# Count build of a graph network kernel: turns of two tiles in a ring of four one-hot places, tile bounds read in two halves

## What is computed

```
dst = sort(int(3125 * uniform**2)), src = randint(0, 3125)      # 50000 edges
x = layernorm(x + gcn(x))            # 128 -> 512 -> 128, symmetric normalisation
x = layernorm(x + gine(x, edge_attr_32))   # edge MLP input, two batch norms
x = layernorm(x + sage(x))           # two mean aggregations
x = layernorm(x + pna(x))            # 3 layers: max, min, std, var per target, 3 scalers
```

## Time and profile before

| | us |
|---|---|
| median of 3 runs | 3185.71 (3182.45 to 3189.19) |
| the profiled execution | 3187.43 |
| its span, first to last instruction | 3185.6 |
| mean granted TensorE clock | 0.849 |
| count build: first L1620 weight load to last L1641 matmul | 33.06 to 434.6 |

### The profile page before, as it was taken

One profiled execution on the slowest core, in us unless ns is written; L12 is line 12 of the kernel. 1 busy time (PEld: TensorE's weight loads), 2 busy tenths in 40 slices (PEclk: granted clock), 3 DMA queues, 4 the chain that ended last, 5 costly groups with the idle time before them and its releaser, 6 DMA issues.

```text
span 3185.6 us, 49509 instructions
## 1 busy us (share of the span) xinstructions
PE 2330.5 (73%) x11826; PEld 1326.7 (42%) x11873; DVE 2185.1 (69%) x6856; ACT 659.8 (21%) x1425; POOL 1274.1 (40%) x1321
## 2 busy tenths in 40 slices
PE   7999869998896988766566767666667676666681
PEld 3444335674563655433333444333334443333351
DVE  8998777557427244766666787666668876666786
ACT  0345551342103010300000043111111421111112
POOL 4000000000200000577777706777775077777740
PEclk9999989999897999878777789777778887777795
DMA  3123347536641543665565406665663166656521
GB/s 134 62 103 124 145 163 258 182 112 216 210 166 64 194 146 113 199 196 196 196 198 194 145 10 227 194 197 194 195 198 114 60 208 196 197 192 197 193 79 41
DMA packets 151716, 510.46 MB, mean 160 GB/s; under 512 B 32178, under 2 KB 51280, under 8 KB 150720
## 3 DMA queue, kind: packets, MB, share of 16 engines
q1 hardware_dynamic: 94254, 348.65, 31.3%
q0 software_dynamic: 43536, 93.43, 11.1%
q10 hardware_dynamic: 13826, 67.12, 5.2%
HBM read 278.95 MB, written 230.13 MB: 160 GB/s over the span
## 4 chain that ended last, share of the span: by engine, by line
PE 28%; DVE 24%; issue 16%; POOL 14%; DMA 11%; ACT 3%; DVEq 2%; ACTq 0%; POOLq 0%
POOL rows_g L671 14%; PE psum L1680 11%; DMA rows_g<-a_dram,idx_now 9%; PE psum L1620 8%; DVE run L853 4%; DVE run L1158 3%; DVE run L1155 2%; PE psum L1913 2%; DMA at_part<-part_now 2%; PE psum L1629 1%; DVE var_tmp L1097 1%; PE psum L1891 1%; PE psum L1752 1%; DVE hs L1204 1%; PE psum L1761 1%
## 5 line engine op out<-in xcount | busy, mean ns | idle before, releaser
L671 POOL DMA_INDIRECT rows_g<-a_dram,idx_now x1173 | 1138.8, 971 | 974.7 <-DMA a_dram<-g 618.1
L1680 PE MATMUL psum<-hs,slab 128*128 128x384 bf16 x6600 | 1174.2, 340 | 55.5 <-DVE hs L835 52.0
L1680 PEld LDWEIGHTS psum<-hs,slab 128*128 128x128 bf16 x6600 | 672.3, 102 | 581.7 <-issue 189.7
L1155 DVE SCALAR_TENSOR_TENSOR run<-run,mask_pt,rows_g 128x128 f32<-128x128 f32 x1170 | 406.0, 347 | 374.9 <-DMA rows_g<-a_dram,idx_now 330.5
L1158 DVE SCALAR_TENSOR_TENSOR run<-run,mask_pt,rows_g 128x128 f32<-128x128 f32 x1170 | 403.6, 345 | 0.1
L1851 PE MATMUL psum<-identity,std_now 128*128 128x128 f32 x75 | 33.9, 452 | 483.8 <-ACT std_now L1513 483.8
L1620 PE MATMUL psum<-onehot_key,onehot_lane 128*128 128x512 bf16 (+1 forms) x1921 | 347.6, 335 | 10.6 <-issue 8.0
L782 DVE TENSOR_SCALAR onehot_key<-key_row,key_at 128x1600 bf16<-128x1600 f16 x492 | 310.1, 630 | 0.0
L1513 ACT ACTIVATE std_now<-var_now,eps 128x128 f32<-128x128 f32 x75 | 30.1, 401 | 1242.7 <-DVE var_now L1117 1242.7
L1620 PEld LDWEIGHTS psum<-onehot_key,onehot_lane 128*128 128x128 bf16 x1968 | 157.3, 98 | 185.6 <-DVE onehot_key L782 20.3
L1851 PEld LDWEIGHTS psum<-identity,std_now 128*128 128x128 f32 x75 | 13.3, 178 | 509.8 <-ACT std_now L1513 509.3
(11 more groups left out here) (319 smaller groups left out, 2742.0 us busy)
## 6 DMA issues: line engine op xcount, KB each, us to landing
slab<-at_part SPq DMA_DIRECT2D x200, 800.0 KB, 4.6
scan_dram<-run SPq DMA_DIRECT2D x291, 512.0 KB, 2.9
at_part<-part_now ACTq DMA_DIRECT2D x50, 800.0 KB, 4.0
sums_dram<-run ACTq DMA_DIRECT2D x43, 576.0 KB, 2.8
rows_g<-a_dram,idx_now POOLq DMA_INDIRECT x1173
rows_g<-in_attr SPq DMA_DIRECT2D x43, 148.5 KB
a_dram<-g SPq DMA_DIRECT2D x15, 320.0 KB, 2.5
agg<-sel_dram SPq DMA_DIRECT2D x3, 1600.0 KB, 8.4
```

What stands on the lines that cost most here:

```text
L671: nc.gpsimd.indirect_dma_start(rows_g[:, slot, j, :], None, a_dram, bass.IndirectOffsetOnAxis(ap=idx_now[:, slot, j:j + 1], axis=0)).then_ ...
L1155: V.scalar_tensor_tensor(at[:, 0:D], before[:, 0:D], mark, rows, ALU.add, ALU.max).then_inc(s_run, 1)
L1680: T_.matmul(ps[:, 0:3 * D], counts[:, k * P:(k + 1) * P], hs[:, k, at:at + 3, :].rearrange("p s f -> p (s f)"), start=(k == 0), stop=False ...
```

## The change

Turns have two tiles, and the ring has four places instead of three. Turn i uses places 0 and 1 where i is even and 2 and 3 where it is odd. DVE, too, now computes the address of what it writes from a register, and PE computes the addresses of both operands of every matmul of the count build from one. `s_tile` starts at 4. The rounding becomes (n/2 + 1/4) to the nearest, with at least 2 turns. For the drawn inputs this gives 234 turns, 468 tiles: 58, 24, 20, 16, 14, 14, 12, 12, 12, five windows of 10, nine of 8 (windows 14 to 22), then 6 or 8, and 4 in the last two; windows 0 to 22 have 304 tiles where they had 321. PE reads 26 bounds before the first window and 26 more between windows 24 and 25, and frees the registers as it goes.

```diff
-TW = 3
+TW = 2
+PLACES = 4
...
+        key_places = onehot_key[:].rearrange("p q k -> p (q k)")
+        lane_places = onehot_lane[:].rearrange("p q k -> p (q k)")
+
+        def place_of(turn, j):
+            return (turn & (PLACES // TW - 1)) * TW + j
...
-            pool.sem_inc(s_tile, TW)
+            pool.sem_inc(s_tile, PLACES)
...
-            step(V.tensor_scalar(steps[:], steps[:], 1.0 / TW, 1.0 / 3, ALU.mult, ALU.add))
+            step(V.tensor_scalar(steps[:], steps[:], 1.0 / TW, 0.5 - 0.5 / TW, ALU.mult, ALU.add))
...
                     dve.wait_ge(s_tile, TW * i + (j + 1))
-                    V.tensor_scalar(onehot_lane[:, j, :], lane_row[:], lane_at[:, ds(at, 1)], None, ALU.is_equal)
-                    V.tensor_scalar(onehot_key[:, j, :], key_row[:], key_at[:, ds(at, 1)], None,
+                    place = place_of(i, j)
+                    V.tensor_scalar(lane_places[:, ds(place * P, P)], lane_row[:], lane_at[:, ds(at, 1)], None,
+                                    ALU.is_equal)
+                    V.tensor_scalar(key_places[:, ds(place * KEYS, KEYS)], key_row[:], key_at[:, ds(at, 1)], None,
                                     ALU.is_equal).then_inc(s_oh, 1)
...
-            regs = [pe.alloc_register(f"start_{w}") for w in range(NW + 1)]
+            HALF = -(-NW // 2)
+
+            def starts(first, n):
+
+                regs = [pe.alloc_register(f"start_{first}_{w}") for w in range(n + 1)]
+                pe.load(regs, ranges[0:1, first:first + n + 1])
+                return regs
+
             pe.wait_ge(s_ranges, 1)
-            for lo in range(0, NW + 1, 26):
-                part = slice(lo, min(NW + 1, lo + 26))
-                pe.load(regs[part], ranges[0:1, part])
+            regs = starts(0, HALF)
...
                     pe.wait_ge(s_oh, TW * m + (j + 1))
+                    place = place_of(m, j)
                     for lo, hi in chunks:
-                        mm = T_.matmul(psum[:, 2048 * h + lo:2048 * h + hi], onehot_lane[:, j, :], onehot_key[:, j, lo:hi],
-                                       start=(start and j == 0), stop=False, skip_group_check=True)
+                        mm = T_.matmul(psum[:, 2048 * h + lo:2048 * h + hi], lane_places[:, ds(place * P, P)],
+                                       key_places[:, ds(place * KEYS + lo, hi - lo)], start=(start and j == 0), stop=False, skip_group_check=True)
...
+            for first in (0, HALF):
+                n = min(HALF, NW - first)
+                if first:
+                    regs = starts(first, n)
+                lo = start_of(regs[0])
+                for w in range(n):
+                    hi = start_of(regs[w + 1])
+                    window((first + w) // 2, (first + w) % 2, lo, hi, first + w == 0)
+                    pe.free_register(regs[w])
+                    lo = hi
+                pe.free_register(regs[n])
```

More of the change, by code:

```diff
@@ L224, in gnn_kernel @@
         lane_at = sbb("lane_at", [P, LT], F32)
-        onehot_key = sbb("onehot_key", [P, TW, KEYS], BF16)
-        onehot_lane = sbb("onehot_lane", [P, TW, P], BF16)
+        onehot_key = sbb("onehot_key", [P, PLACES, KEYS], BF16)
+        onehot_lane = sbb("onehot_lane", [P, PLACES, P], BF16)
+        key_places = onehot_key[:].rearrange("p q k -> p (q k)")
+        lane_places = onehot_lane[:].rearrange("p q k -> p (q k)")
+        def place_of(turn, j):
+            return (turn & (PLACES // TW - 1)) * TW + j
         part_now = [sbb(f"part_now{i}", [P, NB * P], BF16) for i in range(2)]
@@ L1644, in _, with start_of @@
             pe.wait_ge(s_const, N_CONST)
[L1646 to L1653, removed]
+            def start_of(reg):
+                return nc.s_assert_within(pe.snap(reg, donate=True), 0, LT // TW)
+            for first in (0, HALF):
[9 more added lines that the diff above has]
+                pe.free_register(regs[n])
             pe.wait_ge(s_part1, NW + 1)
```

## The result

The changed kernel takes 3278.56 us (3276.68 to 3282.27), the kernel before, beside it, 3185.15 (3182.45 to 3189.19): ratio 1.0294, interval 1.0276 to 1.0311, +93.4 us. I had predicted 3258, with a range of 3182 to 3390. The profiled execution took 3282.27 us, with a span of 3280.4 against 3185.6.

The account below looks back on a forecast made before the run. It took DVE to bound the kernel before and PE's sequencer the changed one: 53.5 + 131.3 + 290.2 = 475.0 us against 401.5, +72.2 with the bounds, 3259.6 profiled, less 1.7 for the median: 3258 us, range 3182 to 3390.

Parts of the forecast that it names:

- PE's sequencer sets the pace: Count build: PE's register instructions, at 0.93 us a tile, exceed DVE's 0.706; chance 0.55, 3205 to 3330 us.
- Six register instructions at 0.115 and half of 0.49, 0.93 a tile: PE's loop of two tiles: 0.69 us of register instructions and 0.24 of loop for each tile; bounds 0.68 to 1.39.
- 2.68 us for a window besides its tiles: Windows 1 to 49: 2.0 us until ACT's copy allows the subtraction, plus its 0.68, covering the first two tiles; 131.3 us.
- A late block of 12.8 us: Late windows: a block takes 2 x (2.68 + 4 x 0.93) us, over the 11.4 of ACT and the store.
- The bounds, 3.6 us gained and 2.3 given back: Register loads: earlier start, then a stop between windows 24 and 25; net -1.3 us, range -3.6 to +3.6.
- 0.6 us in every window where ACT's copy is no longer covered: First turns: two tiles (1.4 us) don't cover the 2.0 us to the subtraction, so PE stands 0.6 us a window.
- DVE's registers cost nothing: DVE's tiles: one or two more register instructions, 0.06 us each, hidden by its engine; at most 0.1 us a tile otherwise.
- After the stage only the shift: Behind the count build: nothing changes but the later start, a microsecond in the stage being one of the total.
- my +72.2 for the stage: Count build: 475.0 us instead of 401.5, +73.5, and +72.2 with the bounds.
- the sequencer keeps up: Rival: PE's register instructions are fewer than counted or overlap; +3.6 us, 3191 us in total; chance 0.17.
- The 0.06 us for each operand with a register address: Rival: each of a tile's eight loads and matmuls also pays a sequencer gap; 1.39 us a loop tile, 3444 us; chance 0.20.
- Faster: Rival: the deeper ring hides PE's first-turn stop, 24 saved tiles count in full, -16.9 us; 3165 us; chance 0.08.

Follow-up runs that it names:

- e1: Kernel before, turns of three and three places kept, but PE takes both operands of each matmul by register, bounds in two halves: ratio 1.022, +84.8 us.
- e5: Kernel after, but all four matmuls of a tile use one key address, so PE has 3.5 register instructions a tile instead of 6.5: ratio 1.0051, +15.2 us.
- e11: Kernel after, but PE's turn stands twice with constant addresses and two branches on the turn's lowest bit choose: ratio 1.0045, +15.8 us.
- e6: Kernel after with the lane one-hot written 512 columns wide instead of 128, about 0.10 us more DVE work a tile: ratio 1.0253, +91.4 us.
- e3: Kernel before with only the bounds read in halves, 26 before window 0 and 26 between windows 24 and 25: ratio 0.9989, -4.7 us.
- e9: Kernel before with its bounds read in parts of 32 and 19 instead of 26 and 25, the second from element 32: 3181.46 us, ratio 0.9988.
- e4: Kernel after with turns of three tiles and a ring of six places, rounding to turns as in before: ratio 1.0237, +76.6 us.
- e10: Kernel before with constant addresses, bounds in halves and five more PE register instructions a tile that no matmul uses: ratio 1.0096, +35.0 us.
- e12: Kernel before reading the first 32 bounds before window 0 and the other 19, from element 32, between windows 30 and 31: ratio 0.997, -13.0 us.

## Why the prediction was right, and where its steps were off

The side, the stage and the mechanism were right. The size owes something to luck: a tile was priced too low and a window's fixed part too high. By an estimate from the figures below, the first would have put me 37 us too low (0.10 in 56 + 312 loop tiles), and the second gave 22 back (0.46 in 49 windows). Each point by its step:

- **PE's sequencer sets the pace: shown** by e1 (the registers alone bring most of the loss), by e5 and e11 (taken away, the loss goes) and by e6 (DVE is off the path).
- **Six register instructions at 0.115 and half of 0.49, 0.93 a tile: the mechanism was right, the size too small.** Measured 1.02 to 1.03. One instruction more in each turn of two (13 for the tiles, I had 12): in the turn's first tile the AND that takes the lowest bit stands alone, unfused. And 1.58 us for the 13 is 0.122 each, not 0.115, since fused instructions with more operations take longer. The loop was 0.45, not 0.49. In windows 0 to 22 this is most of the miss: window 0 took 58.8 us (first weight load 26.51, closing matmul 85.28) where I had 53.5.
- **2.68 us for a window besides its tiles: too high, by some 0.5.** Windows 1 to 22 took 256.8 us where my sum gave 246.8. With 1.03 for 0.93 in their 202 loop tiles the sum would be 267, so the fixed part gives 10 back, 0.46 each. I had put the subtraction's 0.68 us on the sequencer's path. Its four matmuls stand at constant addresses, so the sequencer can issue them and go on to the next turn's registers while PE works on them. The timeline of after shows it, with no idle time between the subtraction and the next tile. Up to the subtraction ACT's copy and the sequencer take the same time: the copy's last instruction ends at 191.16 in the record, the sequencer's wait for it at 191.20, and that wait held it up by some 0.1 us.

```profile
189.57 1.50 ACT L1339 ACTIVATE part_now<-psum 128x1600 bf16<-128x1600 f32 x1 [8.22 <-PE psum L1656]
...
190.66 0.56 PEld L1635 LDWEIGHTS psum<-onehot_key,onehot_lane 128*128 x4 [0.17 <-issue]
...
191.33 0.56 PEld L1644 LDWEIGHTS psum<-part_now,minus_one 128*128 128x128 bf16 x4
...
192.01 0.79 PEld L1635 LDWEIGHTS psum<-onehot_key,onehot_lane 128*128 x5
```

- **A late block of 12.8 us: right, by two errors that cancel.** Two windows of six tiles take 12.5 to 12.8 us, one pair 13.3. My terms as measured (2.68 - 0.46 = 2.22) give 2 x (2.22 + 4 x 1.03) = 12.7: the tiles were 0.8 too low and the fixed parts 0.9 too high. ACT's waits for its store fell from 30.5 to 19.5 us, as they must where PE is later.
- **The bounds, 3.6 us gained and 2.3 given back: both terms mis-sized, the net inside its range but of the other sign.** Measured 6.6 us (33.06 to 26.51) and 8.1 us (window 25 took 14.43, a window of six tiles 6.3): net +1.5, not -1.3. The one long load moved whole, with its whole length, as e3 shows. My reason for halving it, code that must come in either way, was wrong; what matters is which elements the load takes (e9). And the mid-run stop has a tail that I did not think of (below).
- **The term that I priced right:** 0.6 us in every window where ACT's copy is no longer covered: 0.56 in e11. In after itself it doesn't show (2.2 us of such waits in the whole stage), because the sequencer takes as long over two tiles as ACT over its copy.
- **DVE's registers cost nothing: right** (e4 against e1). Its two lines have 2.5 register instructions a tile where they had two; I had said about one more.
- **After the stage only the shift: right**, 3.0 us of the 94.8 between the profiled executions lie elsewhere.

The terms add up: window 0 +5.3, windows 1 to 22 +10.0, windows 23 to 49 +1.5, bounds +2.8, together 19.6 more than my +72.2 for the stage, which gives the +91.8 measured.

Of the rivals, "the sequencer keeps up" fell with the first trace. The 0.06 us for each operand with a register address fell with e5. The Trainium skill, TensorE: Matmul & The Clock Gate, section Wait — 56ns, not 53.3ns?, gives some 62 ns for a matmul that the sequencer's own code decodes, and says nothing of where the address comes from. Here an ALU instruction with a load and matmul behind it is followed by the next register instruction after 0.113 us, with register addresses in after and with constant ones in e10 alike, and after 0.09 to 0.10 without them. So the pair adds some 0.02 us, the register address nothing to it, and the trace speaks for the path that goes past that code, with register addresses too. "Faster" fell too: even without the address arithmetic (e11) turns of two lose 16 us.

## What to carry to other kernels

- Before an operand's place comes from a register, count what the sequencer must do for it: here every distinct address was a fused register instruction, about 0.12 us, and four chunks of one place were four addresses. With the other 2.5 register instructions of a tile they set the pace, at 1.02 us a tile where DVE needs 0.71; one address for all four, or one body for each place with a branch between them, doesn't.
- A turn is not only a unit of waste. The first turn's length is also the cover for another engine's copy, and here one tile less of it ate up the tiles saved (e5 and e11).
- Test an improvement's ceiling first: the change with its overhead taken out (e11) was still slower than before.

## What the runs showed of the hardware that I had not expected

- The time of a load of registers from SBUF depends on which elements it takes: 2.3 us for 26 or 32 registers from element 0, 1.9 and 2.7 for 19 from element 32, but 5.9 to 7.2 for 25 or 26 from element 25 or 26, in all traces. Other starts were not tried, so whether it is 32, 16 or 8 that counts stays open. So does whether it is the start at all: the long loads are also the only ones that reach from below element 32 to above it.
- The load in mid-run cost after 8.1 us, more than its own 6.16. The weight load of window 24's closing matmul starts at 357.15, the next one at 364.50, 7.36 us later where other windows have 0.83. That leaves 1.6 us behind the stop. PE had stood idle (7.57 us by the row below, though the records of the first two matmuls are missing), and then the granted clock was 0.50, the lower of its two levels (1.2 GHz), from 364.9 to 366.9. It was 0.64 in the mean up to the close of the window and 1.00 behind it (PE, PEld, DVE, ACT, POOL, clock). Matmuls there took up to 634 ns, the median is 379. No run tests whether the clock alone makes the 1.6 us.

```profile
364.91 2.39 PE L1635 MATMUL psum<-onehot_key,onehot_lane 128*128 x6 [7.57 <-issue]
...
363.00:371.80 8.80, 6.89 (x29) 3.10 (x31) 3.39 (x10) 2.71 (x5) 0.00 (x0) 0.64 0.00 0
371.80:392.90 21.10, 16.89 (x93) 8.60 (x93) 15.15 (x41) 10.48 (x13) 0.00 (x0) 1.00 0.31 129
```

- A branch of PE's sequencer has two lengths, 0.07 and 0.21 us, by whether it goes on or jumps: in e11 one of the two branches is short and the other long in each of the 234 turns. In the loop of after it is the 0.215.
- The same kernel took 3185, 3722 and 3682 us on three chips, while windows 1 to 24 took 209.0, 209.3 (e3) and 209.5 (e12). What differs behind them was not looked into.
